# An RWKV and mixture-of-experts layer: one logarithm for two divisors, and a new order on four engines

## The chip, the cores and the metric

One core of a Trainium2 chip runs the kernel. The metric is the device time of one execution in microseconds. Five instruction queues work side by side on the core: TensorE (PE, matrix products and transposes), VectorE (DVE), ScalarE (ACT), GpSimd (POOL, here also the issuer of indirect transfers) and SyncE (SP, here only an issuer of plain transfers). Each runs its instructions in the order in which they are written, and a wait on a semaphore holds everything behind it in the same queue.

## The reference, cut to what matters

```python
h = two_wavelet_low_passes(x)                  # 32 sequences, 750 -> 192 steps, 256 channels
k = xn @ Wk.T; r = xn @ Wr.T; v = r            # xn = layernorm(h)
# the recurrence, for each channel, over the 192 steps:
ww = u + kt; q = max(pp, ww)
e1 = exp(pp - q); e2 = exp(ww - q)
y = (e1 * a + e2 * vt) / (e1 * b + e2)
ww2 = pp + w; q2 = max(ww2, kt)
a, b, pp = exp(ww2-q2)*a + exp(kt-q2)*vt, exp(ww2-q2)*b + exp(kt-q2), q2
out = sigmoid(r) * y                           # = y / (1 + exp(-r))
h = h + out @ Wo.T
# then a mixture of 8 experts with 2 chosen by a router, on layernorm(h):
h = h + sum over the 2 chosen experts of gate * (relu(z @ W1 + b1) @ W2 + b2)
```

What the change touches is the last line of the recurrence and the one behind it: both the divisor of y and the 1 + exp(-r) of the sigmoid divide the same numerator.

## The kernel before, in words

The first stage takes the 32 sequences two at a time: 16 pairs of 384 tokens. For each pair SyncE loads the frames (1.5 MB in four transfers, two buffers). TensorE makes both low passes as one product with a band matrix (`conv`). ScalarE copies the result out of PSUM (`hidden_in`), VectorE takes statistics (`statistic_1`, `mean_1`, `shift_1`), ScalarE the root and the normalised rows (`root_1`, `norm_1`). TensorE transposes them (`transpose_1`, copied by `xnT_in`) and makes k and r in four products (`kr` 0 to 3). ScalarE copies these to kpad and v; GpSimd fills the first column of each (`first_key`, `first_value`). The recurrence over the steps is done by scans on VectorE: `running_max`, then `difference`; on ScalarE `distances`, `decays` and `now` make the exponentials; on VectorE `weights_sum` and `weighted_sum` are the two running sums, `divisor` and `numerator` add the step itself, with `value_now` for its value. The division is done in logarithms: ScalarE takes the logarithm of each divisor (`log_sigmoid`, `log_divisor`), VectorE adds them (`log_sum`), ScalarE takes exp of minus the sum (`inverse`), VectorE multiplies (`output`). TensorE adds the product with Wo to h in PSUM (`carry`, `project`). A second normalisation follows (`statistic_2`, `mean_2`, `root_2`, `shift_2`, `h1_from`, `norm_2`, `transpose_2`, `x2T_in`), then `logits` and the choice of two experts in some two dozen operations of 24 or fewer elements on VectorE (`lg_in` to `second_slots`), with `ranks` on TensorE and `gate` on ScalarE between them. GpSimd scatters each pair's tokens to the lists of the experts, six transfers of one column each, and SyncE stores h1 (`put_h1`) and the normalised rows with their gates (`put_rows`, which waits for `second_gate`).

The pairs run as a pipeline of six steps. `rounds` calls each engine's `body` 21 times; in round i the argument p0 is pair i, p1 pair i-1, and so on to p5. The order within each body is written out by hand, one order for each engine, and the step at which a function stands says which pair it works on in that round.

From pair 7 on, `first_lists`, `first_rows` and the like fetch and prepare the first tiles of the second stage, while the first stage still runs; `first_weights` on ScalarE and VectorE split the first expert's weights into a high and a low part.

The second stage goes over 31 tiles of 512 or 256 tokens, each of one expert: two layers of float32 products done as three products of high and low parts. It begins when every engine has left the first stage.

Of the kernel before, what the change touches and what calls it, by code (L numbers as in the profile page):

```python
# [16 lines left out]

# [14 lines left out]
P = 128  # L32
# [37 lines left out]
FILL = 12  # L70
# [8 lines left out]
EMAX = 2.0 ** 54  # L79
CAP = 2.0 ** 55  # L80
# [121 lines left out]
def tokens_to_experts(nc, x, taps, taps_down, wkT, wrT, woT, decay, first, rw, rb, ew, out, rows, lists, tables):  # L202
# [12 lines left out]
    with ctx:  # L215
# [18 lines left out]
        c_eps = sb("c_eps", [P, 1])  # L234
# [20 lines left out]
        lnd, lner, lsum = den, er, den  # L255
# [46 lines left out]
        STATE = {name: n + 1 for n, name in enumerate(('sigmoid_divisor', 'weighted', 'weights_sum', 'divisor', 'weighted_sum', 'log_sum', 'value_now', 'numerator'))}  # L302
        N_LN1, N_LN2, N_DIFF, N_EXP, N_STATE, N_INV, N_CHOICE = 7, 7, 2, 3, len(STATE), 3, 15
        AT_DECAYS = 1
# [7 lines left out]
        def _(sp):  # L312
# [52 lines left out]
        def _(pool):  # L365
# [13 lines left out]
            pool.memset(c_eps[:, :], EPS).then_inc(pads, 1)  # L379
            pool.memset(es[:, 0, :, 0:1], 0.0).then_inc(pads, 1)  # L380
# [3 lines left out]
            pool.wait_ge(pads, 7)  # L384
# [35 lines left out]
            def body(p0, p1, p2, p3, p4, p5):  # L420
                if p5 and not p5.last:
                    fetch.scatter(p5, range(3, 6))
                if p0:
                    first_key(p0)
                if p4 and p4.q == KNOWN:
                    first_lists()
                if p4 and p4.q == KNOWN + 1:
                    first_rows(t0, range(0, 3))
                if p4 and p4.q == KNOWN + 2:
                    first_rows(t0, range(3, R))  # L430
                    first_rows(t1, range(0, 2))
                if p4 and p4.q == KNOWN + 3:
                    first_rows(t1, range(2, R))
                if p4 and p4.q == PAIRS - 4:
                    second_weights()
                if p4 and not p4.last:
                    fetch.scatter(p4, range(3))
                if p0:
                    first_value(p0)
# [4 lines left out]
        def _(act):  # L444
# [70 lines left out]
            def sigmoid_exp(q):  # L515
                act.wait_ge(kr_taken, q.at(4, 4))
                if q.q:
                    act.wait_ge(state, q.at(N_STATE, STATE['log_sum'] - N_STATE))
# [24 lines left out]
            def log_sigmoid(q):  # L543
                act.wait_ge(state, q.at(N_STATE, STATE['sigmoid_divisor']))
                act.activation(lner[:, :, :], er[:, :, :], ACT.Ln).then_inc(inv_ready, 1)

            def log_divisor(q):
                act.wait_ge(state, q.at(N_STATE, STATE['divisor']))
                act.activation(lnd[:, :, :], den[:, :, :], ACT.Ln).then_inc(inv_ready, 1)

            def inverse(q):
                act.wait_ge(state, q.at(N_STATE, STATE['log_sum']))
                act.wait_ge(o_ready, q.at(1))
                act.activation(inv[:, :, :], lsum[:, :, :], ACT.Exp, scale=-1.0).then_inc(inv_ready, 1)
# [11 lines left out]
            def body(p0, p1, p2, p3, p4, p5):  # L566
                if p2:
                    distances(p2)
                if p0:
                    hidden_in(p0)  # L570
                if p2:
                    decays(p2)
                if p5 and p5.last:
                    first_weights(5)
                if p2 and p2.last:
                    first_rows(1)
                if p1:
                    xnT_in(p1)
                if p0:
                    root_1(p0)  # L580
                if p2:
                    log_sigmoid(p2)
                if p5 and p5.last:
                    first_weights(6)
                if p2 and p2.last:
                    first_weights(3)
                if p2:
                    now(p2)
                if p1:
                    kr(p1, 0)  # L590
                if p3:
                    root_2(p3)
# [3 lines left out]
                if p5 and p5.last:  # L596
                    first_weights(7)
                if p3:
                    norm_2(p3)
                if p2 and p2.last:  # L600
                    first_weights(4)
                if p1 and p1.last:
                    first_weights(1)
                if p2:
                    log_divisor(p2)
                if p4:
                    gate(p4)
                if p0:
                    norm_1(p0)
                if p1:  # L610
                    kr(p1, 2)
                if p3:
                    x2T_in(p3)
                if p1 and p1.last:
                    first_weights(2)
                if p0 and p0.last:
                    first_weights(0)
                if p1 and p1.last:
                    first_rows(0)
                if p1:  # L620
                    kr(p1, 3)
                if p2:
                    inverse(p2)
                if p1:
                    sigmoid_exp(p1)
# [4 lines left out]
        def _(pe):  # L630
# [109 lines left out]
            def body(p0, p1, p2, p3, p4, p5):  # L740
                if p2:
                    kr(p2, 3)
                if p4:
                    transpose_2(p4)
                if p0:
                    conv(p0)
                if p5:
                    ranks(p5)
                if p3:
                    carry(p3)  # L750
                if p1 and p1.last:
                    first_rows(1)
                if p4:
                    logits(p4)
                if p1:
                    transpose_1(p1)
                if p3:
                    project(p3)
                if p1:
                    if p1.q == 0:  # L760
                        pe.wait_ge(loaded, 16 * 5)
                    kr(p1, 0)
                    kr(p1, 1)
                    kr(p1, 2)
                if p0 and p0.last:
                    first_rows(0)
# [4 lines left out]
        def _(dve):  # L771
# [29 lines left out]
            dve.wait_ge(pads, 7)  # L801
# [281 lines left out]
            def body(p0, p1, p2, p3, p4, p5):  # L1083
                if p5:
                    second_gate(p5)
                    first_slots(p5)
                if p4:
                    lg_in(p4)
                if p5 and p5.q == KNOWN - 1:
                    first_places_of_tiles()  # L1090
                if p3 and p3.last:
                    first_rows(0)
                if p5 and p5.last:
                    first_weights(6)
                if p5:
                    second_slots(p5)
                if p5 and p5.q == KNOWN - 1:
                    first_experts()
                if p4:
                    best(p4)  # L1100
                if p2:
                    sigmoid_divisor(p2)
                if p4:
                    is_best(p4)
                if p5 and p5.q == KNOWN - 1:
                    first_groups()
# [751 lines left out]
```

## Time and profile before

| what | value |
|---|---|
| three runs | 971.69, 975.03, 980.67 us; median 975.03 |
| the profiled execution | 978.66 us, of which the span of its instructions is 976.9 |
| first matmul of the expert stage | at 318.9 us |
| mean granted TensorE clock | 0.972 |
| busy: PE, DVE, ACT, POOL | 94%, 79%, 63%, 56% of the span |

The span is counted from the first to the last instruction; all positions below are microseconds from its start. About a third of it is the first stage. Busy time over the whole span mixes two stages with different limits, so the share of an engine is read stage by stage.

### The profile page before, as it was taken

To read this page: it belongs to the slowest core of one execution; us is meant where nothing else is said; L and a number is where in the kernel's file an instruction comes from. 1 tells how busy PE (TensorE), PEld (TensorE's weight loads), DVE (VectorE), ACT (ScalarE), POOL (GpSimd) and SP (SyncE) were. 2 spreads that over 40 slices of the span, in tenths; PEclk is the share of its full clock that TensorE was granted. 3 is DMA by queue.
4 is the path that set the end of the run, shared out by engine and by line. 5 is a ranking of instruction groups with operands and counts; after the bars stand their busy time and mean duration, and the time that the engine had idled before them with its cause. 6 is when DMAs were issued, how large, how long until landed. Compare 5 with 4: busy or idle time off the path is not lost. (4 is left out here: it accounts for less than half of the span.)

```text
span 976.9 us, 17356 instructions
## 1 busy us (share of the span) xinstructions
PE 917.9 (94%) x5838; PEld 782.1 (80%) x5838; DVE 776.0 (79%) x2020; ACT 614.7 (63%) x1182; POOL 548.9 (56%) x463
## 2 busy tenths in 40 slices
PE   5799999999965999999999999999999999999996
PEld 3466767676744898899989988998999999999996
DVE  2599999999987776777867878797787778878774
ACT  1799999999973454555655545564565555556552
POOL 1102555567775646555656764675675677467553
PEclk8999999999976899999999999999999999999999
DMA  9743535364231345454546655556564665655633
GB/s 305 242 146 115 182 117 182 117 209 140 70 139 56 133 128 145 134 133 132 144 140 188 174 135 138 139 150 216 142 148 135 164 200 139 144 139 149 214 48 37
DMA packets 73297, 144.33 MB, mean 148 GB/s; under 512 B 9069, under 2 KB 62430, under 8 KB 69242
## 3 DMA queue, kind: packets, MB, share of 16 engines
q0 software_dynamic: 31136, 99.92, 38.0%
q1 hardware_dynamic: 42074, 43.30, 13.7%
q8 instruction: 48, 0.79, 0.3%
q14 instruction: 39, 0.32, 0.1%
HBM read 111.36 MB, written 31.83 MB: 147 GB/s over the span
## 5 line engine op out<-in xcount | busy, mean ns | idle before, releaser
L1452 ACT ACTIVATE hid<-hp,b 128x512 f32<-128x512 f32 (+1 forms) x248 | 158.7, 640 | 263.7 <-PE hp L1489 221.9
L1501 PE MATMUL acc<-whi,hhi 128*128 128x256 f32 x876 | 245.8, 281 | 0.0
L1501 PE MATMUL acc<-wlo,hhi 128*128 128x256 f32 x876 | 245.6, 280 | 0.0
L1501 PE MATMUL acc<-whi,hlo 128*128 128x256 f32 x876 | 245.3, 280 | 0.0
L1406 POOL DMA_INDIRECT out_rows<-yout,dest x108 | 183.3, 1697 | 42.2 <-issue 32.9
L1778 DVE CAST hhi<-hid 128x512 fp32r<-128x512 f32 (+1 forms) x240 | 102.8, 428 | 120.6 <-ACT hid L1452 110.7
L1489 PE MATMUL hp<-xhi,whi 128*128 128x512 f32 (+1 forms) x496 | 186.6, 376 | 8.5 <-PEq L215 4.3
L1489 PE MATMUL hp<-xlo,whi 128*128 128x512 f32 (+1 forms) x496 | 183.8, 371 | 0.0
L1489 PE MATMUL hp<-xhi,wlo 128*128 128x512 f32 (+1 forms) x496 | 183.3, 370 | 0.0
L1501 PEld LDWEIGHTS acc<-wlo,hhi 128*128 128x128 f32 x876 | 165.3, 189 | 8.4
L1501 PEld LDWEIGHTS acc<-whi,hhi 128*128 128x128 f32 x876 | 164.6, 188 | 8.0
L1535 DVE TENSOR_TENSOR wlo<-h,whi 128x512 fp32r<-128x512 f32 x240 | 162.8, 684 | 3.0 <-ACT whi L1432 3.0
L1501 PEld LDWEIGHTS acc<-whi,hlo 128*128 128x128 f32 x876 | 165.1, 189 | 0.0
L1432 ACT ACTIVATE whi<-h 128x512 fp32r<-128x512 f32 x240 | 147.8, 624 | 19.0 <-DMA h<-in_ew,idx 19.0
L1780 DVE TENSOR_TENSOR hlo<-hid,hhi 128x512 fp32r<-128x512 f32 (+1 forms) x240 | 152.3, 635 | 8.3
L184 POOL DMA_INDIRECT h<-token_rows,tile_tid x110 | 120.7, 1097 | 62.3 <-issue 62.3
L169 POOL DMA_INDIRECT expert_lists<-tokens,slots x96 | 121.8, 1268 | 35.6 <-issue 23.0
L1489 PEld LDWEIGHTS hp<-xhi,whi 128*128 128x128 f32 x496 | 93.9, 189 | 18.6 <-DVE xlo L1051 4.4
L1489 PEld LDWEIGHTS hp<-xlo,whi 128*128 128x128 f32 x496 | 93.8, 189 | 16.4
L178 POOL DMA_INDIRECT tile_tid<-expert_lists,idx x31 | 32.8, 1059 | 122.6 <-DVE idx L189 109.7
L1489 PEld LDWEIGHTS hp<-xhi,wlo 128*128 128x128 f32 x496 | 94.1, 190 | 8.8
L388 POOL TENSOR_TENSOR kpad<-kpad,c_before 128x4 f32<-128x4 f32 x16 | 6.3, 396 | 114.3 <-ACT kpad L468 114.3
(219 smaller groups left out, 1474.3 us busy)
## 6 DMA issues: line engine op xcount, KB each, us to landing
frames<-in_x SPq DMA_DIRECT2D x32, 512.0 KB
frames<-in_x SPq DMA_DIRECT2D x32, 256.0 KB
token_rows<-xs SPq DMA_DIRECT2D x16, 388.5 KB
out_rows<-h SPq DMA_DIRECT2D x16, 384.0 KB
expert_lists<-setup SPq DMA_DIRECT2D x12, 280.0 KB
h<-token_rows,tile_tid POOLq DMA_INDIRECT x110
out_rows<-yout,dest POOLq DMA_INDIRECT x110
expert_lists<-tokens,slots POOLq DMA_INDIRECT x96
```

The lines of the kernel that those rows point to most:

```text
L169: self.pool.indirect_dma_start(self.lists, bass.IndirectOffsetOnAxis(t.slots[:, q.q, c:c + 1], 0), t.tokens[:, q.q, c % 3, :], None).then_ ...
L178: self.pool.indirect_dma_start(t.tid[:, j.s, 0:j.r, :].rearrange("p r a -> p (r a)"), None, self.groups[j.r], bass.IndirectOffsetOnAxis(t. ...
L184: self.pool.indirect_dma_start(t.xg[:, j.s, r, :], None, self.rows_of[0:upto, :], bass.IndirectOffsetOnAxis(t.tid[:, j.s, r, 0:1], 0)).the ...
L388: pool.tensor_tensor(kpad[:, q.s, :, 0:1], kpad[:, q.s, :, 1:2], c_before[:, :, :], ALU.add).then_inc(seeded, 1)
L1406: pool.indirect_dma_start(out[:, :], bass.IndirectOffsetOnAxis(dest[:, j.i, r:r + 1], 0), yout[:, j.s, r, :], None, compute_op=ALU.add).th ...
L1432: act.activation(whi[j.s][:, a], raw[:, j.s, a], ACT.Copy).then_inc(whi_done, 1)
L1452: act.activation(hid[:, c % 2, 0:j.r * P], hp[c % 2][:, 0:j.r * P], ACT.Relu, bias=b1[:, j.s, c:c + 1]).then_inc(hid_done, 1)
L1489: last = pe.matmul(hp[c % 2][:, 0:j.r * P], w_[j.s][:, at:at + P], x_[j.s][:, k, 0:j.r * P], start=n == 0, stop=n == 3 * HC - 1)
L1501: last = pe.matmul(acc_of(j, r), h_[:, c % 4, r * P:(r + 1) * P], w_[j.s][:, at:at + C], start=c == 0 and n == 0 and (r % 2 == 0 or j.last ...
L1535: dve.tensor_tensor(wlo[j.s][:, a], raw[:, j.s, a], whi[j.s][:, a].bitcast(F32), ALU.subtract).then_inc(wlo_done, 1)
L1778: dve.tensor_copy(hhi[:, c % 4, 0:j.r * P], hid[:, c % 2, 0:j.r * P]).then_inc(hhi_done, 1)
L1780: dve.tensor_tensor(hlo[:, c % 4, 0:j.r * P], hid[:, c % 2, 0:j.r * P], hhi[:, c % 4, 0:j.r * P].bitcast(F32), ALU.subtract).then_inc(hlo_ ...
```

## The change

The sigmoid's exponential er gets its one from ScalarE (`sigmoid_divisor`, an Identity with a bias tensor that holds 1) and no longer from VectorE; the cap EMAX on er moves into a product er x den on VectorE (`whole_divisor`), which takes the place of the addition of two logarithms. One logarithm is taken of that product, scaled by 1/256, and the last Exp has a bias tensor of -log 256. The caps are smaller (2^35 and 2^36 in place of 2^54 and 2^55), so that the product stays in range. VectorE's `sigmoid_divisor` and ScalarE's `log_sigmoid` are gone.

All five queues are written in a new order. In the core of the diff below stands what changes in kind; VectorE's order is cut to its outline.

```diff
-EMAX = 2.0 ** 54
-CAP = 2.0 ** 55
+EMAX = 2.0 ** 35
+CAP = 2.0 ** 36
+SCALE = 2.0 ** 8
...
@@ SyncE's round
             def body(p0, p1, p2, p3, p4, p5):
-                if p0 and p0.q + 2 < PAIRS:
-                    load(Pair(p0.q + 2))
-                if p5:
-                    put_rows(p5)
+                if p1 and p1.q + 2 < PAIRS:
+                    load(Pair(p1.q + 2))
                 if p3:
                     put_h1(p3)
+                if p4:
+                    put_rows(p4)
...
@@ GpSimd's round, after
+                if p0:
+                    first_key(p0)
+                if p4 and not p4.last:
+                    fetch.scatter(p4, range(3, 6))
+                if p0:
+                    first_value(p0)
+                if p3 and p3.q == KNOWN:
+                    first_lists()
+                if p3 and p3.q == KNOWN + 1:
+                    first_rows(t0, range(0, 3))
...
+                if p3 and not p3.last:
+                    fetch.scatter(p3, range(3))
...
@@ ScalarE's functions
-            def log_sigmoid(q):
-                act.wait_ge(state, q.at(N_STATE, STATE['sigmoid_divisor']))
-                act.activation(lner[:, :, :], er[:, :, :], ACT.Ln).then_inc(inv_ready, 1)
+            def sigmoid_divisor(q):
+                act.wait_ge(er_ready, q.at(2, 1))
+                act.activation(er[:, :, :], er[:, :, :], ACT.Identity, bias=c_unit[:, 0:1]).then_inc(er_ready, 1)
             def log_divisor(q):
-                act.wait_ge(state, q.at(N_STATE, STATE['divisor']))
-                act.activation(lnd[:, :, :], den[:, :, :], ACT.Ln).then_inc(inv_ready, 1)
+                act.wait_ge(state, q.at(N_STATE, STATE['whole_divisor']))
+                act.activation(den[:, :, :], den[:, :, :], ACT.Ln, scale=1.0 / SCALE).then_inc(inv_ready, 1)
...
-                act.activation(inv[:, :, :], lsum[:, :, :], ACT.Exp, scale=-1.0).then_inc(inv_ready, 1)
+                act.activation(inv[:, :, :], den[:, :, :], ACT.Exp, bias=c_scale[:, 0:1], scale=-1.0).then_inc(inv_ready, 1)
...
@@ VectorE's functions
-            def sigmoid_divisor(q):
-                dve.wait_ge(er_ready, q.at(1, 1))
-                dve.tensor_scalar(flat(er[:, :, :]), flat(er[:, :, :]), EMAX, 1.0, ALU.min, ALU.add).then_inc(state, 1)
...
-            def log_sum(q):
-                dve.wait_ge(inv_ready, q.at(N_INV, 2))
-                dve.tensor_tensor(flat(lsum[:, :, :]), flat(lnd[:, :, :]), flat(lner[:, :, :]), ALU.add).then_inc(state, 1)
+            def whole_divisor(q):
+                dve.wait_ge(er_ready, q.at(2, 2))
+                dve.wait_ge(state, q.at(N_STATE, STATE['divisor']))
+                dve.scalar_tensor_tensor(out=den[:, :, :], in0=er[:, :, :], scalar=EMAX, in1=den[:, :, :],
+                                         op0=ALU.min, op1=ALU.mult).then_inc(state, 1)
```

The orders after the change, with the step at which each function stands (its pair in round i is i less that number; the functions that prepare the first tiles are left out but for those named):

- ScalarE: gate 5, hidden_in 0, log_divisor 3, kr2 2, inverse 3, now 2, kr3 2, distances 2, xnT_in 1, decays 2, root_1 0, sigmoid_exp 2, root_2 3, kr0 1, h1_from 3, kr1 1, norm_2 3, sigmoid_divisor 2, norm_1 0, x2T_in 3. For the last pair, first_weights(7) and both first_rows stand behind its gate.
- TensorE: conv 1, transpose_2 5, kr2 3, logits 5, kr3 3, carry 4, transpose_1 2, project 4, kr0 2, kr1 2, ranks 5.
- VectorE: is_first 4, statistic_1 0, other_logits 4, second_slots 5, mean_1 0, second 4, value_now 2, four small ones 4, statistic_2 3, second_number 4, mean_2 3, is_second 4, weighted 2, shift_2 3, selected 4, weights_sum 2, shift_1 0, places 4, divisor 2, running_max 1, new_ends 4, whole_divisor 2, difference 1, weighted_sum 2, lg_in 3, numerator 2, best 3, output 2, then ten small ones, second_gate 4 and first_slots 4 the last.

## Rows read from the trace of the kernel before

**Rows 1.** Busy time by engine in 50 us of the first stage, granted clock, DMA.
```profile
100.00:150.00 50.00, 48.73 (x292) 34.14 (x291) 50.00 (x154) 48.84 (x100) 28.27 (x26) 1.00 0.48 153
```
**Rows 2.** Timeline of VectorE, one round: start, length, operation.
```profile
149.98 0.17 DVE L915 TENSOR_TENSOR lg<-cnt_ps,rbs 128x24 f32<-128x24 f32 x1
...
150.28 0.55 DVE L866 TENSOR_SCALAR er<-er 128x768 f32<-128x768 f32 x1
150.75 0.17 DVE L923 TENSOR_TENSOR eq<-lg,m 128x24 f32<-128x24 f32 x1
150.84 1.07 DVE L825 BATCH_NORM_STATS2 st<-h 128x6 f32<-128x256 f32 x3
...
165.99 0.15 DVE L1071 TENSOR_TENSOR xs<-ed,xs 128x3 f32<-128x3 f32 x1
...
166.15 0.17 DVE L915 TENSOR_TENSOR lg<-cnt_ps,rbs 128x24 f32<-128x24 f32 x1
```
**Rows 3.** Timeline of ScalarE around its idle times, same round.
```profile
155.94 0.48 ACT L468 ACTIVATE kpad<-kr_ps 128x384 f32<-128x384 f32 x1
156.68 1.58 ACT L495 ACTIVATE xs<-h,nb,rs 128x256 f32<-128x256 f32 x3 [0.26 <-DVE nb L844]
...
161.58 0.48 ACT L468 ACTIVATE v<-kr_ps 128x384 f32<-128x384 f32 x1
162.12 0.84 ACT L554 ACTIVATE inv<-den 128x768 f32<-128x768 f32 x1
```
**Rows 4.** ScalarE's groups of instructions, 100 to 280: busy us, mean ns.
```profile
L473 ACT ACTIVATE lv<-mv,c_eps 128x3 f32<-128x3 f32 x21 | 6.0, 287 | 0.8 <-DVE mv L829 0.8
...
L475 ACT ACTIVATE rs<-lv 128x3 f32<-128x3 f32 x21 | 4.3, 204 | 0.7
```
**Rows 5.** Timeline of SyncE's queue: an early load, and one steady round.
```profile
39.42 1.98 SPq L324 DMA_DIRECT2D frames<-in_x  x4
...
162.41 1.99 SPq L324 DMA_DIRECT2D frames<-in_x  x4
166.21 0.37 SPq L340 DMA_DIRECT2D token_rows<-xs  x1
```
**Rows 6.** Timeline of TensorE, the same round.
```profile
152.65 2.74 PE L695 MATMUL kr_ps<-xnT,wk 128*128 128x384 f32 x8
155.23 2.80 PE L695 MATMUL kr_ps<-xnT,wr 128*128 128x384 f32 x8
158.31 0.55 PE L650 MATMUL tp_ps<-ident,xs 128*128 128x128 f32 x3 [0.28 <-ACT xs L495]
...
159.12 3.24 PE L668 MATMUL conv_ps<-frames,setup 128*64 128x256 f32 x28
...
168.81 2.42 PE L695 MATMUL kr_ps<-xnT,wk 128*128 128x384 f32 x7
```
**Rows 7.** DMA traffic from 38 to 50 us in 40 slices, and its one queue.
```profile
GB/s 17 0 0 0 0 0 0 0 119 177 0 24 341 393 382 382 382 386 382 352 345 365 331 352 355 171 3 0 0 0 0 0 0 0 0 27 0 0 0 0
...
q1 hardware_dynamic: 1606, 1.58, 40.5%
```
**Rows 8.** Timeline of GpSimd: three fetched blocks, three scatters, then first_value.
```profile
239.25 1.18 POOL L184 DMA_INDIRECT h<-token_rows,tile_tid  x1 [0.59 <-issue]
...
244.13 1.63 POOL L169 DMA_INDIRECT expert_lists<-tokens,slots  x1 [0.30 <-issue]
...
249.10 0.22 POOL L392 TENSOR_TENSOR v<-v,c_one 128x4 f32<-128x4 f32 x1
```
**Rows 9.** Timeline of TensorE at the start: conv of pair 2.
```profile
34.45 4.93 PE L668 MATMUL conv_ps<-frames,setup 128*64 128x256 f32 x28 [2.85 <-DMA frames<-in_x]
```
**Rows 10.** Timeline of VectorE: its last operation of the first stage.
```profile
317.64 0.68 DVE L1051 TENSOR_TENSOR xlo<-conv_ps,xhi 128x512 fp32r<-128x512 f32 x1
```
**Rows 11.** Timeline of TensorE: idle ahead of the ranks of a late pair.
```profile
259.45 0.17 PE L704 MATMUL cnt_ps<-sel,ones 128*128 128x8 bf16 x1 [2.17 <-DVE sel L977]
```
**Rows 12.** Busy time by stretch, as rows 1, behind that idle time.
```profile
260.00:263.00 3.00, 3.00 (x9) 2.36 (x10) 3.00 (x8) 3.00 (x6) 2.39 (x3) 0.50 0.05 11
```

More of the change, by code:

```diff
@@ L299, in tokens_to_experts @@
         xt = [conv_ps[:, 512 * k:512 * k + TS] for k in range(HC)]
[L302 to L304 removed]
+        STATE = {name: n + 1 for n, name in enumerate(('value_now', 'weighted', 'weights_sum', 'divisor', 'whole_divisor', 'weighted_sum', 'numerator'))}
+        N_LN1, N_LN2, N_DIFF, N_EXP, N_STATE, N_INV, N_CHOICE = 7, 7, 2, 3, len(STATE), 2, 15
+        AT_DECAYS = 3
         def tile_of_h(q, t):
@@ L566, in body @@
             def body(p0, p1, p2, p3, p4, p5):
-                if p2:
-                    distances(p2)
+                if p5:
+                    gate(p5)
+                if p4 and p4.last:
+                    first_weights(3)
                 if p0:
                     hidden_in(p0)
+                if p3:
+                    log_divisor(p3)
+                if p3 and p3.last:
+                    first_weights(1)
+                if p2:
+                    kr(p2, 2)
+                if p4 and p4.last:
+                    first_weights(4)
+                if p3:
+                    inverse(p3)
+                if p2:
+                    now(p2)
+                if p4 and p4.last:
+                    first_weights(5)
+                if p5 and p5.last:
+                    first_weights(7)
+                if p2 and p2.last:
+                    first_weights(0)
+                if p2:
+                    kr(p2, 3)
+                    distances(p2)
+                if p1:
+                    xnT_in(p1)
                 if p2:
                     decays(p2)
[L573 to L578, printed above, removed]
                 if p0:
                     root_1(p0)
+                if p5 and p5.last:
+                    first_rows(0)
                 if p2:
-                    log_sigmoid(p2)
-                if p5 and p5.last:
+                    sigmoid_exp(p2)
+                if p4 and p4.last:
                     first_weights(6)
[L585 to L588, printed above, removed]
+                if p3:
+                    root_2(p3)
                 if p1:
@@ L740, in body @@
             def body(p0, p1, p2, p3, p4, p5):
+                if p1:
+                    conv(p1)
+                if p5:
+                    transpose_2(p5)
+                if p3:
+                    kr(p3, 2)
+                if p5 and p5.last:
+                    first_rows(0)
+                if p5:
+                    logits(p5)
+                if p3:
+                    kr(p3, 3)
+                if p4:
+                    carry(p4)
                 if p2:
-                    kr(p2, 3)
+                    transpose_1(p2)
                 if p4:
-                    transpose_2(p4)
-                if p0:
-                    conv(p0)
+                    project(p4)
+                if p2:
+                    if p2.q == 0:
+                        pe.wait_ge(loaded, 16 * 5)
+                    kr(p2, 0)
+                    kr(p2, 1)
                 if p5:
                     ranks(p5)
-                if p3:
-                    carry(p3)
-                if p1 and p1.last:
+                if p5 and p5.last:
                     first_rows(1)
[L753 to L766, printed above, removed]
             rounds(body)
@@ L1083, in body @@
             def body(p0, p1, p2, p3, p4, p5):
-                if p5:
-                    second_gate(p5)
-                    first_slots(p5)
                 if p4:
-                    lg_in(p4)
+                    is_first(p4)
                 if p5 and p5.q == KNOWN - 1:
[L1090 to L1106, printed above, removed]
-                if p1 and p1.last:
-                    first_weights(0)
-                    taken()
+                    first_weight_rows()
                 if p0:
@@ L1120, in body @@
                 if p4:
-                    first_number(p4)
+                    second(p4)
                 if p2:
-                    weighted(p2)
+                    value_now(p2)
                 if p5 and p5.q == KNOWN - 1:
-                    first_list_rows()
+                    first_numbers()
+                if p5 and p5.last:
+                    first_weights(6)
                 if p4:
-                    is_first(p4)
-                if p3 and p3.last:
-                    first_weights(1)
-                    taken_each()
+                    is_second_best(p4)
+                    margin(p4)
+                    first_expert(p4)
+                    second_numbers(p4)
                 if p3:
@@ L1133, in body @@
                         statistic_2(p3, t)
-                if p5 and p5.q == KNOWN - 1:
-                    first_numbers()
+                if p4 and p4.last:
+                    first_rows(0)
+                    first_weights(2)
+                    region()
                 if p4:
-                    other_logits(p4)
-                if p0:
-                    shift_1(p0)
+                    second_number(p4)
                 if p3:
```

181 lines of the change are left out of this document (87 added, 94 removed).

## The prediction, made before the changed kernel was run

> **What bounds the kernel now.** First the busy time per stretch: between 100 and 150 us VectorE is busy in all 50 us, TensorE and ScalarE in nearly 49, GpSimd in 28 [rows 1]. The expert stage behind it is TensorE's and is not touched, so a microsecond won or lost ahead of it is one of the whole. A busy share alone doesn't say who sets the pace, so next the timeline of single engines, where the distance from one start to the next is what an instruction really takes (it overlaps its follower by about 0.08 us on VectorE, 0.1 on ScalarE). VectorE repeats after 16.17 us (lg at 149.98 and at 166.15) with no idle time between [rows 2]: it is the bound, at 16.17 us a pair. ScalarE idles 0.37 us ahead of xs (kpad at 155.94 gives way after 0.37, xs starts at 156.68) and 0.17 ahead of inv, so its own work is 16.17 - 0.54 = 15.63 us [rows 3]. TensorE's busy 48.7 of 50 us are 15.7 a pair. All three are within 4% of each other: a change that helps one of them can win 0.5 us a pair at most, some 7 us in all.
>
> **VectorE's work.** One TENSOR_SCALAR goes (er, a step of 150.75 - 150.28 = 0.47 us [rows 2]); the addition of the logarithms gives its place to a product of the same size. So VectorE needs 16.17 - 0.47 = 15.70 us. In the new order first_gate and second_gate stand closer than before; about 0.05 for such dependences makes 15.75.
>
> **ScalarE's work.** A logarithm of 768 elements goes, an addition of one of 768 comes, so 0 for the pass itself. But both the addition and the last Exp now read a per-partition bias. The small activations show its price: lv, with a bias tensor, takes 287 ns, rs, without one, 204 ns [rows 4]. Two such biases are 2 x 0.09 = 0.18 us: ScalarE needs 15.63 + 0.18 = 15.81 us, more than VectorE. With everything else on time the pair would take some 15.85 us, 0.32 less than now.
>
> **SyncE's order, where I see the cost.** Each round now issues the load of a pair, then the store of h1, then the store of the rows of the pair four rounds old. The queue is in order, so the load of pair q+6 stands behind put_rows(q), which waits for second_gate(q). Before, it stood behind put_h1(q), and behind the rows of a pair two older, both long done: the load at 162.41 went out as soon as a conv had freed the frames (159.12 and 3.24 long), two rounds before it was wanted [rows 5, 6]. Now count back from statistic_2 of pair q+3, which follows project(q+3), which follows conv(q+6) in TensorE's order. On VectorE second_gate(q) is at the end of one round and statistic_2(q+3) stands 2.8 us into the round after the next (three statistics 0.99 [rows 2], means 0.23, value_now 0.87, the rest small): 15.75 + 2.8 = 18.5 us apart. On TensorE conv to project takes 168.81 - 159.12 = 9.69 before; without ranks (0.16), with transpose_2 (0.81) and two of kr (half of 155.23 - 152.65 for each, 2.58 together) that is 12.9, and 0.2 for the last matmul's end: 13.1 [rows 6]. So conv would have to start 18.5 - 13.1 = 5.4 us after second_gate.
>
> Can the load be there by then? put_rows goes out 0.07 us after second_gate (xs, at 165.99 and 0.15 long, ends at 166.14; the store starts at 166.21) and takes 0.37 to issue [rows 2, 5]. A load issued at 39.42 moves its 1.58 MB until slice 25 of 40 of a 12 us window, that is until 45.8: 6.4 us, 4.4 of them at some 350 GB/s [rows 5, 7]. The rows' 0.39 MB stand in front: 0 to 1.1 us. The semaphore comes after the last byte; no row has that time, I take 0.4 (0.3 to 1.4). So conv starts 0.07 + 0.37 + 6.4 + 1.1 + 0.4 = 8.3 us after second_gate, bounds 7.2 and 9.3. It is 2 to 4 us late, every round.
>
> That closes a loop of one round: after conv (159.12 - 162.30, 3.2 with its follow-on [rows 6]) comes transpose_2, and ScalarE, in order, waits there with x2T of an old pair before it gets to the logarithm and the inverse that output waits for. From second_gate to the next: 8.3, conv 3.2, transpose_2 0.8, end 0.2, x2T 0.4, gate 0.1, hidden_in 0.7, Ln 0.73, kr 0.37, inverse and its end 0.95 [rows 3], output and the ten small operations to second_gate 1.6: **17.4 us**, bounds 16.3 and 18.4. The loop over two rounds, (8.3 + 13.1 + 12.95) / 2 = 17.2, says nearly the same, and with the quick bound 16.6. So each held round costs 17.4 - 16.17 = 1.2 us more than now (0.4 to 2.2). Held are the rounds of the loads 6 to 15, ten of them: **+12.3 us** (4 to 22). The two other rounds between pairs 3 and 15 win 0.3 each: -0.6; the 1.1 us that VectorE's extra work for the first tiles adds today is half hidden in those waits: -0.5.
>
> The Trainium skill, page "DMA: Bandwidth & Descriptors", section "Anatomy of one DMA — SWDGE (gpsimd) path", fits a transfer's time as about 2.0 us plus its bytes over 436 GB/s, for GpSimd's path. An estimate from that page gives 6.5 us for load and rows together. The row of this trace, 6.4 us for the load alone until its last byte, is slower. By the page the two-round loop would be (0.1 + 6.5 + 13.1 + 12.95) / 2 = 16.3 us and the sum some 11 us smaller.
>
> **GpSimd's order.** The scatter of three columns now precedes first_key of the next pair. Three inserted transfers and three scatters took 239.25 to 249.10, 9.8 us [rows 8]; in the rounds in which the first lists and rows are fetched they all stand between first_value and the next first_key, which running_max awaits. From ScalarE's copy of v to running_max I count 8.9 us, so 0 to 2.3 late, in three rounds: up to 5 us where nothing else holds the round. With ScalarE and output already waiting for 1.6 us in the same rounds I take 0 for it.
>
> **Start and end.** kr 2 and 3 of pair 0 now stand behind conv(2), which waits for its load until 34.45 and ends near 39.4 [rows 9]; they ran before it. Carried forward by hand, running_max of pair 3 comes 2.2 us later than now (0 to 4). At the end, VectorE has two more subtractions of 0.6 each behind the last logits (one such, xlo, is at 317.64 [rows 10]) and waits about 1 for ScalarE's high part of x, which stands behind the last gate; the last choice and placement in one round give 1 back in the drain: +0.8 (-1 to +3).
>
> **The sum.** 12.3 - 0.6 - 0.5 + 2.2 + 0.8 = +14.2 us. Against the profiled execution, 978.66 us (span 976.9 and 1.8 around it), that is 992.9; that execution was 3.6 above the median of three, so on the median 975.03 + 14.2 = **989 us**.
>
> **The rivals.**
> The order works (0.18). The load lands within some 5.5 to 6 us, or the pipeline's slack takes up more than I count, and rounds go at 15.85: 12 x 0.32 = 3.8 won, 3.0 lost at start and end, 0 to 5 at GpSimd: 974 to 979, say 976. For it: TensorE, ScalarE and VectorE fit together by my count, if with 0.05 us to spare at statistic_2. Against it: no load in this trace is that quick. It decides at a landing of 5.5 us.
> The load binds, but lightly (0.15). Landing at the quick bound, or as the page has it, 16.3 to 16.6 a round: 4 in place of 12.3, 981.
> The clock falls in the gaps (0.17). TensorE would idle 17.4 - 15.7 = 1.7 us in one piece before each conv. After an idle of 2.17 us that ended at 259.45 the granted clock was 0.50 from 260 to 263, the lower of its two levels [rows 11, 12]. If conv runs so each round it takes 1.7 us more, and conv is in the loop: +17, 1006. Against it: the idle would be shorter than that one, and the steady rounds stand at full clock [rows 1].
> The forecast, 989, has 0.50; its own range is 982 to 996.
>
> **How the numbers follow.** About 1% (9.8 us) is what three runs with a spread of 9 us can tell from no change. Over 984.8: nine tenths of the forecast, the clock's case and a third of the light one: 0.68. Under 965.3 only if start, end and GpSimd all come out at their best: 0.05. The rest 0.27. The range takes in the clock's case and the lower part of "works": 975 to 1006.
>
> **What would show it.** Right: SyncE's load of a steady round starts just behind the store of token_rows; TensorE's conv waits for DMA about 2 us each round from pair 6 on; VectorE idles ahead of oT or st2, released by ScalarE or TensorE, and its round is near 17.4; identity and inverse on ScalarE last 0.09 us longer. Wrong: conv without such a wait, rounds of 15.8, or a wait of running_max for GpSimd's kpad as the largest one.

## The result, and the profile after

The changed kernel takes 1036.99 us (median of four runs, 1030.2 to 1037.7) where the kernel before takes 975.62 in runs beside it: 1.060 times as long, 95% interval 1.056 to 1.065. The forecast was 989 with a range to 1006. Its sign was right, its size short by 48 us.

The expert stage begins with the first product into hp (TensorE's timelines, before and after):

```profile
318.88 0.77 PE L1489 MATMUL hp<-xhi,whi 128*128 128x512 f32 x1 [4.34 <-PEq L215]
```
```profile
379.98 0.77 PE L1490 MATMUL hp<-xhi,whi 128*128 128x512 f32 x1 [3.68 <-PEq L217]
```

That is +61.1 us, the whole loss; the stage itself is 3 us shorter. So the loss lies in the rounds of the pairs. First the busy time by stretch of the changed kernel, to be held against [rows 1]; its columns are PE, PEld, VectorE, ScalarE, GpSimd, granted clock, DMA share and GB/s.

```profile
100.00:150.00 50.00, 40.40 (x235) 27.87 (x234) 41.47 (x115) 39.55 (x81) 22.51 (x21) 0.93 0.40 126
150.00:200.00 50.00, 42.12 (x234) 30.16 (x233) 41.92 (x137) 42.54 (x86) 20.37 (x21) 0.97 0.47 138
200.00:250.00 50.00, 37.05 (x200) 25.53 (x202) 39.80 (x114) 35.37 (x71) 25.54 (x23) 0.85 0.45 149
```

No engine is busy for more than 42.5 of 50 us any more: nothing is bound by work, everything by waits. And the granted clock is below 1. The chain of waits, between 100 and 300 us (total, times, longest), names them:

```profile
ACT x2T L514 <- PE tp_ps L656: 32.0, 10, 8.6
...
DVE lg L920 <- PE cnt_ps L742: 27.0, 9, 8.1
...
PE conv_ps L674 <- DMA frames<-in_x: 21.3, 10, 6.6
PE cnt_ps L710 <- DVE sel L982: 18.0, 10, 1.9
DVE t L887 <- issue: 17.5, 9, 2.0
```

The first three are one chain: conv waits for its frames; transpose_2 stands behind conv, x2T behind that, the logits behind x2T, and lg_in on VectorE behind the logits. The last line is another matter: VectorE's value_now (the product t) waits nearly 2 us in nearly every round, and the view names no releaser for it ("issue" stands where it finds none).

One round, on SyncE's queue, TensorE, ScalarE and VectorE in turn (timelines; start, length, operation, idle time before it). They answer to [rows 2, 3, 5, 6].

```profile
173.48 0.37 SPq L341 DMA_DIRECT2D token_rows<-xs  x1
173.90 2.35 SPq L325 DMA_DIRECT2D frames<-in_x  x4
...
180.86 0.17 PE L710 MATMUL cnt_ps<-sel,ones 128*128 128x8 bf16 x1 [1.78 <-DVE sel L982]
...
182.06 3.24 PE L674 MATMUL conv_ps<-frames,setup 128*64 128x256 f32 x28 [0.91 <-DMA frames<-in_x]
```
```profile
167.81 0.49 ACT L514 ACTIVATE x2T<-tp_ps 128x384 f32<-128x384 f32 x1 [2.12 <-PE tp_ps L656]
...
170.45 0.95 ACT L560 ACTIVATE inv<-den,c_scale 128x768 f32<-128x768 f32 x1
...
182.99 0.93 ACT L551 ACTIVATE er<-er,c_unit 128x768 f32<-128x768 f32 x1
...
185.87 0.49 ACT L514 ACTIVATE x2T<-tp_ps 128x384 f32<-128x384 f32 x1 [0.48 <-PE tp_ps L656]
```
```profile
170.61 0.18 DVE L920 TENSOR_TENSOR lg<-cnt_ps,rbs 128x24 f32<-128x24 f32 x1 [1.65 <-PE cnt_ps L742]
170.71 0.95 DVE L909 TENSOR_TENSOR num<-t,sa 128x768 f32<-128x768 f32 x1
...
173.22 0.16 DVE L1076 TENSOR_TENSOR xs<-ed,xs 128x3 f32<-128x3 f32 x1
...
177.02 0.96 DVE L887 SCALAR_TENSOR_TENSOR t<-ey,v 128x768 f32<-128x768 f32 x1 [2.03 <-issue]
```

Read it as a loop. second_gate ends at 173.38; the store of the rows goes out at 173.48 and the load right behind it, at 173.90; conv starts at 182.06, 8.7 us after second_gate; x2T follows 3.8 us later at 185.87. In the round before, x2T at 167.81 led to lg at 170.61 (2.8) and that to the end of second_gate (2.8). 8.7 + 3.8 + 2.8 + 2.8 = 18.1 us, and it closes on itself.

The scans of the pairs (running_max on VectorE) start 17.9, 17.5, 20.4, 20.2, 18.4, 19.7, 18.1, 20.0, 21.0, 26.2, 21.4, 22.5 and 20.1 us apart, from pair 2 on; before they stand 16.0 to 16.2 apart but for one round of 17.3 and the last of 16.7. The first two, 17.9 and 17.5, are not the load's: conv waits for its frames for the first time at 103.95 us, and then ten times. Of these ten rounds, 207.9 us in all, those of 18.4 and 18.1 are the loop as it was just added up. In the eight others the granted clock falls, as in this window of the round in which conv (162.30) took 4.93 us in place of 3.24:

```profile
163.00:166.00 3.00, 3.00 (x18) 1.72 (x16) 3.00 (x4) 2.68 (x5) 2.69 (x2) 0.50 0.25 83
```

0.50 is the lower of the clock's two levels, 1.2 GHz. Before, it never stood there between 38 and 259 us. conv takes 1.7 us more, it is in the loop, and 18.1 becomes 19.8 (the four such rounds ahead of the fetches take 19.7 to 20.4). The round of 26.2 is one in which GpSimd fetches lists and the first expert's weights (start of the fetch at 235.20) just as the exposed load (232.90) is under way; conv got its frames 13.9 us after the load's first issue, against 8.2 in the round shown. SyncE's queue, GpSimd, TensorE, and the busy time by stretch:

```profile
232.90 2.38 SPq L325 DMA_DIRECT2D frames<-in_x  x4
...
235.20 0.94 POOL L176 DMA_INDIRECT h<-in_ew,idx  x1 [0.30 <-issue]
...
246.76 5.69 PE L674 MATMUL conv_ps<-frames,setup 128*64 128x256 f32 x28 [6.57 <-DMA frames<-in_x]
```
```profile
240.00:244.00 4.00, 0.19 (x6) 0.09 (x4) 4.00 (x5) 4.00 (x9) 3.21 (x4) 0.69 1.05 437
```

### The profile page after: what moved, and what is told of

It reads as the page before. It is cut to its first block and busy times, and to the rows that moved or that the text cites. A ratio compares the mean times of both kernels' runs of the same rounds, so it can differ in the third digit from the quotient of the medians.

```text
span 1034.7 us, 17359 instructions
## 1 busy us (share of the span) xinstructions
PE 933.7 (90%) x5838; PEld 795.2 (77%) x5838; DVE 771.0 (75%) x2004; ACT 617.3 (60%) x1182; POOL 539.0 (52%) x465
## 5 line engine op out<-in xcount | busy, mean ns | idle before, releaser
L1502 PE MATMUL acc<-whi,hlo 128*128 128x256 f32 x876 | 245.5, 280 | 0.0
L186 POOL DMA_INDIRECT h<-token_rows,tile_tid x110 | 118.4, 1076 | 60.7 <-issue 60.7
L171 POOL DMA_INDIRECT expert_lists<-tokens,slots x96 | 117.7, 1226 | 44.6 <-issue 22.2
L1490 PEld LDWEIGHTS hp<-xlo,whi 128*128 128x128 f32 x496 | 94.0, 189 | 16.2
L1490 PEld LDWEIGHTS hp<-xhi,whi 128*128 128x128 f32 x496 | 93.9, 189 | 15.9 <-issue 4.1
L674 PE MATMUL conv_ps<-frames,setup 128*64 128x256 f32 x448 | 71.2, 486 | 32.5 <-DMA frames<-in_x 32.5
```

The source lines that it names most:

```text
L171: self.pool.indirect_dma_start(self.lists, bass.IndirectOffsetOnAxis(t.slots[:, q.q, c:c + 1], 0), t.tokens[:, q.q, c % 3, :], None).then_ ...
L186: self.pool.indirect_dma_start(t.xg[:, j.s, r, :], None, self.rows_of[0:upto, :], bass.IndirectOffsetOnAxis(t.tid[:, j.s, r, 0:1], 0)).the ...
L674: last = pe.matmul(conv_ps[half * REST:(half + 1) * REST, t * C:(t + 1) * C], weights, xin[:, q.s, b, block, :], start=n == 0, stop=n == l ...
L1490: last = pe.matmul(hp[c % 2][:, 0:j.r * P], w_[j.s][:, at:at + P], x_[j.s][:, k, 0:j.r * P], start=n == 0, stop=n == 3 * HC - 1)
L1502: last = pe.matmul(acc_of(j, r), h_[:, c % 4, r * P:(r + 1) * P], w_[j.s][:, at:at + C], start=c == 0 and n == 0 and (r % 2 == 0 or j.last ...
```

## The experiments

There are four theories. The load: its place behind the store of the rows makes the whole loss, as forecast, only larger. The order: something in the new order other than the load holds rounds too; the 2 us ahead of value_now are its mark. The arithmetic: it costs by itself (bias operands, place of the logarithm). The clock: its falls cost time of their own. The expectations number their theories with letters, each for itself. Times of rounds, of scans and of hp are those of one profiled execution for each kernel; the totals and their intervals are of all its runs.

**The load back in front, all else changed.**

```
 def body(p0, ...):                      # SyncE
-    if p1 and p1.q + 2 < PAIRS:
-        load(Pair(p1.q + 2))
+    if p0 and p0.q + 2 < PAIRS:
+        load(Pair(p0.q + 2))
```

> The changed kernel with one thing put back: the load of a pair stands again in its old round of SyncE's order, so it no longer waits behind the store of the rows. Theory A (the load behind put_rows is the cause, the slow clock follows from TensorE's wait for it): conv waits for no transfer, rounds of 15.8 to 16.2 us, 970 to 982 us in all. Theory B (the new orders of TensorE, ScalarE and VectorE don't fit together either): rounds stay over 17, over 995 us. Theory C (GpSimd's scatters ahead of first_key): running_max waits for kpad in the three rounds in which rows are fetched, 1 to 2.5 us each, and the total is up to 5 us above what A says.

Measured: 1003.54 us, 1.028 (1.023 to 1.033) times before. conv waits for no frames any more, the clock falls twice between 62 and 280 us, and more than half of the loss is gone (hp starts at 343.7). But most rounds are 17.47 us (the expectations below say 17.45), not 15.85, and those of the two falls 18.8. So the load isn't the whole loss; what is left stands in the timelines of this run, VectorE first, then ScalarE:

```profile
112.55 0.14 DVE L952 TENSOR_REDUCE m<-lg 128x3 f32<-128x24 f32 x1
114.18 0.96 DVE L887 SCALAR_TENSOR_TENSOR t<-ey,v 128x768 f32<-128x768 f32 x1 [1.48 <-issue]
...
116.47 0.30 DVE L846 BATCH_NORM_AGGREGATE mv<-st 128x2 f32<-128x6 f32 x3
```
```profile
108.43 1.13 ACT L547 ACTIVATE ey<-dl,u 128x384 f32<-128x384 f32 x2
...
112.58 1.51 ACT L539 ACTIVATE es<-dist 128x1536 f32<-128x1536 f32 x1
...
116.80 0.30 ACT L479 ACTIVATE lv<-mv,c_eps 128x3 f32<-128x3 f32 x1 [1.56 <-DVE mv L846]
...
130.05 1.51 ACT L539 ACTIVATE es<-dist 128x1536 f32<-128x1536 f32 x1
```

t starts 0.09 us after es ends, though it does not read es. It reads ey, which was done 4.6 us before. The reason is in value_now's wait, a line that the change does not touch:

```
dve.wait_ge(exps, q.at(N_EXP, N_EXP))
```

exps counts the three exponentials of a pair (decays makes one, now makes two), and the line waits for all three. Before, decays (es) was the first of them; the change makes it the last (AT_DECAYS goes from 1 to 3). So the same line, which used to mean "ey is there", now means "es is there". That closes a loop: es, then t, then statistic_2 and mean_2 behind it in VectorE's queue, then root_2 on ScalarE (the operation lv), which waits 1.56 us, then all that ScalarE has between root_2 and the next es. From es to es it is 17.47 us, of which ScalarE is busy for 17.47 - 1.56 = 15.91.

**SyncE's order alone**, in the kernel before: its load, h1 and rows in the changed kernel's order and labels, nothing else.

> The kernel before with nothing but SyncE's new order. In its own TensorE order conv of pair q+6 starts 9.2 us after second_gate(q), and a load behind the store of the rows was landed 8.7 us after it in the changed kernel. Theory A (what decides is the distance from second_gate to conv): rounds of 16.2 to 16.5, 974 to 985 us. Theory D (a load behind a store costs 2 us or more in any order): rounds of 17 and more, over 990 us.

Measured: 980.07 us, 1.004 (1.001 to 1.007). The rounds from pair 3 on are 16.1 to 16.5, but for one of 17.3, which before has too, one of 17.7 and the last of 15.8. conv waits for frames five times between 80 and 250 us, 1.7 at most. SyncE's order does little harm by itself: hp starts at 319.8 in place of 318.9. In the old order of the engines second_gate comes early enough for it: in the round in which it ends at 166.7 conv starts at 176.1, 9.3 us later, and without a wait. It takes the two orders together.

**The new arithmetic alone**, in the orders of before (sigmoid_divisor on ScalarE, whole_divisor in place of log_sum, one log_divisor just ahead of inverse).

> The kernel before in its own orders with the new arithmetic alone: the one added by ScalarE, one product, one logarithm just ahead of the last Exp. VectorE saves 0.47 us a pair, ScalarE needs 0.18 more of its 0.54 us of idle time. Theory A: rounds of 15.7 to 15.9 us, 967 to 972 us. Rival: ScalarE, with the logarithm, its end and the Exp in a row behind the product, keeps output waiting: rounds of 16.1 and more, no gain.

Measured: 981.63 us, 1.005 (1.003 to 1.008). Rounds of 16.58 us with ScalarE waiting up to 0.8 for whole_divisor ahead of the logarithm. By itself the arithmetic costs half a per cent (0.3 to 0.8).

**TensorE kept at work** in the changed kernel, by 24 dummy products a round while it waits for the ranks and the frames.

> The changed kernel with 24 small products of constants a round in TensorE's queue where it otherwise idles, 16 ahead of the wait for ranks and 8 ahead of the wait for the frames; they go to the bank that conv overwrites, and their result is used nowhere. If half the clock after the idle time is a cost of its own: fewer stretches at half clock, steady rounds of 18.1 to 18.5 in place of 18 to 21, 1005 to 1025 us. If it only fills time in which TensorE would wait anyway: 1034 to 1040 us.

Measured: 1040.32 us, 1.060 (1.055 to 1.064). The stretches at 0.50 are still there (103.2 to 106.6, 123.6 to 127.0, 144.0 to 151.0 us and so on). The products did not keep the clock up, so this run says nothing of what the clock costs.

**Both mended**: the load back in front, and value_now waiting for what it reads.

```
-    dve.wait_ge(exps, q.at(N_EXP, N_EXP))
+    dve.wait_ge(exps, q.at(N_EXP, 2))
```

> The changed kernel with the load back in its old round and, besides, value_now waiting for the second of the three counts of exps in place of the third. With the load put back alone, rounds of 17.45 us are left, in which value_now idles 1.5 to 2.0 us until decays (es) is done, though it reads only what now (ey) makes: before the change decays was the first of the three, now it is the last, and the number in value_now's wait stayed at three. Theory E (that wait is the second cause): rounds of 15.8 to 16.0 us where no first rows are fetched, 965 to 976 us in all. Rival F (something else holds the round just behind, as ranks behind sel or the root behind mean_2): rounds over 16.8, over 990 us. Theory C (GpSimd): running_max waits 1 to 2.5 us for kpad in three rounds.

Measured: 986.24 us, 1.004 (1.001 to 1.008). The rounds are 15.9 us, 0.3 better than before, where nothing is fetched: the loss of the loops is gone. The rounds with fetches take 16.5 to 17.3. The rounds came as expected, the total didn't: the profiled execution took 990.06 us, at the upper end of ten runs from 978.2 to 990.9, and in it the stretch from the first product into hp to the 501st takes 239.9 us, against 231.4 before. There ScalarE waited 5.3 us until 341.4, with the releaser named as remote (3.7 in such a wait before), while the DMA moved 388 GB/s between 335 and 340.

**value_now's wait alone mended**, the load still behind the rows.

> The changed kernel with value_now's wait lowered to the second count alone; the load stays behind the store of the rows. If the load alone sets a loop of 17.4 to 18.4 us, as the prediction has it: rounds of 17.4 to 18.4 at full clock, longer where the clock falls, 1000 to 1025 us. If the two causes don't add up because they share one loop: as the changed kernel, 1030 to 1040. If the wait was the larger cause: under 1000.

Measured: 1032.76 us, 1.054 (1.048 to 1.060). Nearly nothing is won: hp starts at 374.8 in place of 380.0, while the same line brings it from 343.7 to 321.0 where the load is in front. Now conv alone waits, longer (TensorE's timeline of this run):

```profile
142.00 4.93 PE L674 MATMUL conv_ps<-frames,setup 128*64 128x256 f32 x28 [4.09 <-DMA frames<-in_x]
...
162.96 4.90 PE L674 MATMUL conv_ps<-frames,setup 128*64 128x256 f32 x28 [3.79 <-DMA frames<-in_x]
```

From 100 to 228 us a stretch at 0.50 stands in every round, each time with such a wait of 3.0 to 4.1 us ahead of conv, and every conv takes 4.8 to 4.9. The rounds are 20.2 to 21.3.

**A third of each load**, in the changed kernel and in the one with value_now's wait mended. SyncE's order and all waits stay; two thirds of the frames are not loaded, and conv reads old ones in their place.

```
 for lo, n in ((0, K_FIRST), (K_FIRST, K_REST)):
+    n = 1 if q.q >= 2 else n
```

> The changed kernel, with each load from pair 2 on cut to a third of its bytes (one block of 128 frames of each part in place of four and two; 0.52 MB in place of 1.57; the other frames that conv reads are old ones, so this leaves work of the computation out). SyncE's order, the four transfers of a load and all waits are the changed kernel's. At the 350 to 390 GB/s that the load shows there the last byte comes 2.7 to 3.0 us sooner. If the load's landing behind put_rows makes the round (18.0 to 20.4 us, up to 26.2 with fetches), the rounds fall by about that much and stop at the 17.45 us of value_now's own loop, conv's waits for the load are nearly gone, most of the stretches at half clock go, and the time is 1003 to 1010. If it is rather the issue behind second_gate and a transfer's fixed time, or the order of the engines, then a third of the bytes changes little: above 1025.

> The same cut of the loads, with value_now waiting for the second exponential only. If the two loops are all that the change costs, the rounds come to 16 to 17.5 us, by the loop 20.2 - 3.0 = 17.2 with the half clock in it and about 16 without, and the time to 983 to 995. If something else of the orders holds the rounds, they stay at 17.5 or more as in the run beside it and the time above 1000.

Measured: 1004.44 us (1.021, 1.015 to 1.028) and 990.53 us (1.007, 1.002 to 1.011). The rounds are 17.47 in the first and 15.9 in the second where nothing is fetched, the same two figures as with the load in front, and conv waits for no frames. So it is the time until the last byte that held conv, not the issue behind second_gate, which is as late here as there. And without the late load the clock stays up: one fall between 75 and 258 us in the first, none between 48 and 265 in the second. The 1.6 us a round between 15.9 and 17.47 are value_now's. In the first run, too, a round with a fall takes 18.8 in place of 17.5.

**GpSimd's order of before**, in the kernel with both mends and in the changed kernel.

> The kernel with both mends (load of a pair at the head of SyncE's round, value_now waiting for the second exponential only), and with GpSimd's order of before: the scatter of the second choice ahead of first_key, the first fetches and the scatter of the first choice between first_key and first_value. With both mends and GpSimd's new order the rounds were 15.9 us where nothing is fetched, and 16.9, 17.3, 17.0 and 16.6 in the four rounds with fetches. If GpSimd's new order makes these four long, they come back to 15.9 to 16.2 here and the expert stage begins 3 to 4 us earlier, near 317.5 in place of 321.0; the time is 983 by the same expert stage as there, or 973 to 976 if the ten microseconds which its expert stage lost came from that order too. Rival: the four rounds are long because of VectorE's extra work for the first tiles (before has 17.3 in one round for it): then hp starts at 321 as there and the time stays 986.

> The changed kernel with GpSimd's order of before and nothing else undone. Its rounds from pair 11 on were 21.0, 26.2, 21.4, 22.5 us against 17.5 to 20.4 ahead of them, with conv waiting for its load for up to 6.6 us. If GpSimd's new order puts the fetches into the same stretch as the exposed loads, these rounds fall to about 20 and the time to 1025 to 1030. If the loads are exposed to any fetch, wherever GpSimd issues it, the same microseconds come in other rounds and the time stays within 5 us of 1037.

Measured: 982.57 us, 1.001 (0.998 to 1.004), and 1036.83 us, 1.058 (1.053 to 1.062). In the first the rounds with fetches fall to 15.9 to 16.3 behind one of 16.9, and hp starts at 319.0 in place of 321.0. The 501st product comes 229.3 us after the first, 10.6 less than with GpSimd's new order. That doesn't show a gain of the order: this execution took 978.00 us, 4.6 under the median of its kernel, the other 990.06, 3.8 over its own, and the median of 982.57 is what was expected for an expert stage that is not shorter. In the second no round is 26 us long, but nearly all are 20.3 to 22.7: hp starts at 377.2 in place of 380.0, and the total stays. The best mend is as fast as before and no faster, though in its steady stretch no engine has slack:

```profile
100.00:150.00 50.00, 49.19 (x292) 34.80 (x293) 50.00 (x148) 49.81 (x101) 28.16 (x25) 1.00 0.50 147
```

**The product early**, in the orders of before with the new arithmetic: whole_divisor directly behind divisor.

> The orders of before with the new arithmetic, as in the run of one logarithm alone (981.6, rounds of 16.58 us, ScalarE waiting 0.8 us for the product ahead of the logarithm), but VectorE makes the product directly behind divisor instead of behind weighted_sum and four small operations. If that wait is what makes ScalarE's round 16.58, it goes and the round falls to 15.8 or 16.2: the time is 976 to 970. If ScalarE's own work with its two bias operands and its other waits fill the round, the wait for the product goes and nothing is won: 980 to 982.

Measured: 985.90 us, 1.003 (1.001 to 1.006). ScalarE's wait for the product is gone and most rounds fell from 16.58 to 16.1 to 16.2. But the round between the scans of pairs 14 and 15 (259.9 and 280.4) takes 20.4 with the clock at 0.50 for half of it (261.4 to 271.6), a second such stretch follows (281.8 to 292.0), and hp starts at 327.9, in place of 325.2. The steady rounds are better by 0.4, and nothing is gained in all. Neither case of the expectation came true. The trace is of one of the longer executions, 993.99 us, so its late falls say little of the median.

**Where the 61 us lie.** For the runs with and without the two loops: the scan of pair 3, the twelve rounds to that of pair 15, and from there to hp.

| run | scan of pair 3 | 12 rounds | to hp | hp |
|---|---|---|---|---|
| before | 78.6 | 195.6 | 44.7 | 318.9 |
| changed | 87.2 | 245.5 | 47.3 | 380.0 |
| load in front | 85.6 | 212.3 | 45.8 | 343.7 |
| value_now's wait alone | 83.2 | 246.6 | 45.0 | 374.8 |
| both mended | 81.2 | 194.8 | 45.0 | 321.0 |
| both, old GpSimd order | 81.0 | 193.8 | 44.2 | 319.0 |
| old GpSimd order alone | 86.2 | 243.7 | 47.3 | 377.2 |
| a third of the load | 83.4 | 212.2 | 46.3 | 341.9 |
| a third, value_now's wait | 80.2 | 198.2 | 45.8 | 324.2 |

The two loops do not add. Against the kernel with both mends, at the start of hp value_now's costs 22.7 us by itself (343.7 - 321.0) and the load's 53.8 (374.8 - 321.0); together they cost 59.0, and 2.1 of the 61.1 are left with both mends. While conv's frames are late, value_now waits in the load's shadow.

## Why the prediction was right or wrong

Right, **the mechanism of SyncE's queue**: the load goes out 0.5 us after second_gate, conv waits for it in each of the ten rounds from pair 6 on, and x2T, gate and lg_in wait behind conv. The term from second_gate to conv was put at 8.3 us (7.2 to 9.3). It is 8.7 in the round shown and up to 9.2 in the first six of the ten held rounds, but 9.8 to 14.4 in the last four. The fit of the Trainium skill, page "DMA: Bandwidth & Descriptors", section "Anatomy of one DMA — SWDGE (gpsimd) path", gave 6.5 us for rows and load; here it was 8.6 from the rows' issue (173.48) to conv (182.06), and 14.3 in the round with the fetch. The trace does not agree, and the loop by the page's figure would have been 2 us too short. The fit is stated for GpSimd's path and for one transfer; these are five, and SyncE's.

Right, **the size of the ramp's own part**: +2.2 was forecast, and with both mends the scan of pair 3 comes 2.5 to 2.6 late. In the changed kernel it is 8.6, and 4.0 of these are value_now's, by the run in which its wait alone is mended (83.2 against 87.2).

Right, **the biases**: inverse takes 0.95 in place of 0.84, the added Identity 0.93. ScalarE needs 15.91 us a round (forecast 15.81), and rounds without loops are 15.9 (forecast 15.85). The end's term, +0.8 (-1 to +3), came out as +2.6 in the changed kernel and as -0.5 to +0.3 with both mends, inside its bounds.

Wrong, and the step that the result turns on: **the cost of the held rounds**, the term of +12.3 us for ten rounds of 17.4 us each at full clock. The ten rounds in which conv waits took 207.9 us, 20.8 each, and that is +46.2 against ten of 16.17. Worked out from the rows above, the 33.9 us over ten of 17.4 are an estimated 7 for a loop of 18.1, 14 for the lower clock in eight of them at 1.7 each, and 13 for the rest of the last four rounds, those with fetches. The two other rounds, which were to win 0.3 each, take 1.3 and 3.9 more than 16.17. The three steps behind this term are taken one by one below, after a fourth that was left out of the forecast altogether. (The lower bound of a held round's cost, 0.4, goes with the 16.6 of the loop over two rounds; the 16.3 given beside it would make 0.1. Nothing hangs on it.)

Wrong, a wait that was left out: **what value_now waits for**. The count back from statistic_2 had value_now as 0.87 us of work, and ScalarE's need was taken as its pace "with everything else on time". I looked at what value_now reads, not at what it waits for. With its wait on the third count the floor of a round is 17.47 us even with the load in front, and 16.3 to 16.6, the lower bound and the light rival, could not happen; nor could "the order works". That this floor is so near the forecast's 17.4 is chance. By itself this cause is worth 22.7 us, more than the whole forecast; behind the late load, as the change has it, mending it wins only 5.2 of the 61.1.

Wrong by a term: **the loop of the load**. I let it run through inverse and output (3.25 + 1.6 us behind x2T's start, by the forecast's terms). But lg_in stands ahead of numerator and output in VectorE's order, and waits for logits, behind x2T: 2.8 + 2.8, which is 0.75 more. With 0.4 more for the landing and 0.4 less from conv to x2T (3.8, forecast 4.2) that makes 18.1 of 17.4.

Wrong by a chance: **the clock** had 0.17 and an idle time of 1.7 us, measured against the one late idle time of before [rows 11, 12]. The idle time is 1.8 ahead of ranks plus 0.9 to 6.6 ahead of conv, the clock fell in eight of the ten held rounds, and it costs the 1.7 us a round that the rival named. The forecast kept it apart from the loop's length; without the late load it nearly vanished (one fall between 75 and 258 us with a third of the load, two between 62 and 280 with the load in front). No run took the clock's fall away and left the late load, so its share in the 61 us is argued and not shown: it rests on the lengths of conv (4.93 and 3.24) and on rounds with and without a fall in one trace (20.4, 20.2, 19.7 and 20.0 against 18.4 and 18.1 here, 18.8 against 17.47 with the load in front).

Wrong by a term: **rounds with fetches** (21.0 to 26.2 us, 0 forecast). I had asked whether GpSimd's small seeds come late. What comes late is the load itself: in the round of 26.2 the fetch of weights shares the DMA with it, as the rows show; for the three others that is argued. As long as a load is a round early, as before, conv doesn't wait for it; exposed, it made conv wait up to 6.6 us, 5.7 more than in the round shown. The run with GpSimd's old order adds that the place of the fetches matters little then. With both mends GpSimd's new order may still cost some 2 us at the start of hp (321.0 against 319.0); its interval (1.001 to 1.008) and that with the old order (0.998 to 1.004) overlap, so the total doesn't show it.

Open: whether the 8.5 us that the mended kernel's expert stage lost at its start belong to the kernel or to that one execution, and what held it there. That the shorter rounds bring no gain is seen in the table: with both mends and the old GpSimd order the twelve rounds win 1.8 us and the end 0.5, and the ramp loses 2.5.

## What to carry to other kernels

A count on a shared semaphore names an order, not a value: whoever moves one of the producers has to read every wait on it again, in functions the diff does not show too. Ahead of a forecast, list for each operation of the critical engines its waits as well as its operands, and close every loop they make; the longest loop is the round. A transfer issued behind a fresh result in an in-order queue can expose its whole landing time, and then everything else that uses the DMA, and the clock that falls in the idle time, is in the loop as well. What decides is how soon behind that result its reader is due: at 9.3 us the same queue order cost 0.9 us by the start of hp. And of two loops that overlap, mending the shorter shows nothing: value_now's line was worth 5.2 us with the late load and 22.7 without.

## What the hardware showed that was not expected

With waits of 3.0 to 4.1 us ahead of conv the granted clock fell to 0.50 in each of seven rounds in a row, 3.4 us each time; with waits of 0.9 to 1.5 it fell in some rounds and not in others (conv took 4.93 us at 200.28 behind 1.06, and 3.24 at 144.28 behind 1.25). 24 small products a round put into the waiting time did not prevent it. An exposed load of 1.57 MB and rows of 0.39 MB reached their reader 8.6 us after the first issue, and 14.3 with another fetch beside them, at 437 GB/s for all together in the busiest 4 us. With a third of the load's bytes the same queue held no one.
